# A 16-head attention block followed by a mixture of experts, float32 on one core: four heads per stack in row tiles of 32 rows, three score buffers, another order on VectorE and of the last up projections

## The chip, the cores and the metric

One core of a Trainium2 chip. The metric is the device time of one execution in microseconds. Three runs of the kernel before gave 1210.15, 1210.59 and 1213.12 us, median 1210.59.

## What is computed

The input x has 32 batches of 256 tokens with 128 features. Each batch passes a layer norm, attention with 16 heads of 8 features, a residual, a second layer norm, and four experts of 512 hidden features of which each token uses two, and a second residual. The attention weights are no softmax but `s(l - max l)` over its sum:

```python
pos = 1.0 + x * (1.0 + 0.5 * x * (1.0 + x / 3.0))
neg = 1.0 / (1.0 - x * (1.0 - 0.5 * x * (1.0 - x / 3.0)))   # x = logit - row maximum, so always this branch
h = silu(xf @ w1) * (xf @ w3)        # per expert
out = sum_e gates[:, e] * (h @ w2)   # gates: softmax, top 2, renormalized
```

## The kernel before, in words

The program is a software pipeline over batches. `over_batches` (L237) gives every engine, for each n from -2 to 33, a first half and a second half; all engines execute their instructions in the order written, and semaphores tie them together. B = 32 batches, U = 8 score tiles of a batch, G = 4 groups of four heads, UP = 8 units of the up projection (each 2 of the 16 blocks of 128 hidden features), C = 2 blocks of 128 tokens.

**First half of n.** TensorE computes the "distances" of batch n (logit minus row maximum, cubic argument), `distances` (L918), tile by tile, and between them the up projections of batch n-2, each unit u as an `a` part (w1, `up_a_unit`) and a `b` part (w3, `up_b_unit`), six matmuls each at L867. It also makes the values of batch n+1 (L959), the last weighted values of batch n-1 (L883), and turns and projects the attention output of batch n-1 (L979, L990, L998). ScalarE squares each distance tile (`square`, L498) and takes the silu of each `a` part (L506). VectorE forms the cubic `polynomial(u)` (L628) from the square and the distance and multiplies silu and `b` part (`hidden(u)`, L620). GpSimd splits queries and keys into a high and a low part (L393, L396), then waits for `gate_all`, the gates laid over all partitions by DMA, and multiplies the eight hidden units by them (`gate_hidden`, L384): seven in the first half, the eighth in the second half behind the wait for VectorE's layer norm statistics (`agg_ok`, L411). The `a` part has one PSUM bank (`up_a`), the `b` part is in `up_b`, for units 3, 5 and 7 in `pv`.

**Second half of n.** TensorE computes the raw scores of batch n+1 (`scores`, L1013) between the down projections of batch n-2 (`down(e, c)`, L1031, four blocks of an expert by w2, which as float32 are eight matmul records). VectorE takes the negated row minima of each score tile (`scores_max`, L718; the keys carry a minus sign, so these are the maxima), splits them (L769, L771), adds the expert result to the residual (`experts_added`, L744), and forms the router's logits, ranks and gates of batch n-1 (L751 to L805). The maxima are transposed on TensorE (`maxima_T`, L1078), copied out (`maxima_out`, L779), and written by a DMA of the SP queue (L347) into rows of the stacked queries, so that the distance matmul subtracts them. ScalarE does logarithm and exponential of the polynomials (L555, L560); TensorE multiplies the weights by the values (`weighted_values`, L870). At the end come the operand of the router (L1052), the operand and the projection of the queries and keys of batch n+2 (L1060, L1089), and the `a` and `b` part of unit 0.

Heads are stacked over partitions: a stack holds two heads in two halves of 64 rows, of which 60 (score) or all (distance, with the other head's rows of `k_pad` at zero) are used. A score tile has four matmuls, in two row tiles of 64 rows; a distance tile has four matmuls of all 128 rows. The stacks are filled from a scratch tensor in DRAM by the SP queue (12 DMAs a batch, L326 and L333). Scores and distances share two buffers of two PSUM banks each (`sc[:, u % 2, :]`), so a score tile u waits until tile u-2 has been reduced:

```python
pe.wait_ge(s_used, U * m + u - 1)      # scores(u), L1022
pe.wait_ge(hid_ok, UP * (m + 1) - 1)   # down(0, 0), L1037: units 0 to 6 are multiplied
pe.wait_ge(gated, UP * m + FB // 2 * (e + 1))   # down(e, c), L1040
```

VectorE's order in the first half is, for u = 0 to 7: `hidden(0)` ahead of `polynomial(0)`, the copy of the values ahead of `polynomial(1)`, the statistics of the next input ahead of `polynomial(3)`, `normalized` behind `hidden(3)`, `attention_added` ahead of `polynomial(7)`, and `hidden(u)` behind `polynomial(u)`. In the second half: statistics, the eight maxima with `router_T` and `queries_T` ahead of the seventh and `biased_logits` ahead of the eighth, `split_maxima`, `experts_added`, `shifted_logits`, `maxima_out`, `compare`, the copy of queries and keys, the gate steps.

## Time and profile before

| | us |
|---|---|
| median of three runs | 1210.59 |
| the profiled execution's own time | 1212.56 |
| its span, first to last instruction | 1210.8 |
| TensorE matmul busy | 1134.5 (94%) |
| ScalarE busy | 1001.7 (83%) |
| VectorE busy | 997.0 (82%) |
| GpSimd busy | 730.1 (60%) |

The profile is of one execution. Busy shares of TensorE are those of pipelined matmuls, whose records overlap: a group of matmuls is read from the start of one group to the start of the next. "Down pair" and the like below are names of stretches between two such starts. Times within the span count from its first instruction.

### The profile page before, as it was taken

To read this page: it belongs to the slowest core of one execution; us is meant where nothing else is said; L and a number is where in the kernel's file an instruction comes from. 1 tells how busy PE (TensorE), PEld (TensorE's weight loads), DVE (VectorE), ACT (ScalarE), POOL (GpSimd) and SP (SyncE) were. 2 spreads that over 40 slices of the span, in tenths; PEclk is the share of its full clock that TensorE was granted. 3 is DMA by queue.
4 is the path that set the end of the run, shared out by engine and by line. 5 is a ranking of instruction groups with operands and counts; after the bars stand their busy time and mean duration, and the time that the engine had idled before them with its cause. 6 is when DMAs were issued, how large, how long until landed. Compare 5 with 4: busy or idle time off the path is not lost.

```text
span 1210.8 us, 29497 instructions
## 1 busy us (share of the span) xinstructions
PE 1134.5 (94%) x10116; PEld 984.2 (81%) x10116; DVE 997.0 (82%) x1838; ACT 1001.7 (83%) x1001; POOL 730.1 (60%) x959
## 2 busy tenths in 40 slices
PE   2679999999999999999999999999999999999988
PEld 1447888888888888888888888888888888888877
DVE  5778888988888898888889888888988888898732
ACT  1378898888889888888988888998888889888862
POOL 6114666665656666565666656567666565766555
PEclk9988999999999999999999999999999999999999
DMA  5212212222221122222112222211222221122000
GB/s 177 64 62 79 63 51 65 79 84 84 84 63 48 61 78 84 84 83 65 49 59 78 84 84 84 67 55 50 78 84 84 84 68 54 50 78 81 28 23 27
DMA packets 92907, 84.89 MB, mean 70 GB/s; under 512 B 11784, under 2 KB 87240, under 8 KB 92872
## 3 DMA queue, kind: packets, MB, share of 16 engines
q1 hardware_dynamic: 92152, 83.79, 22.0%
q10 hardware_dynamic: 720, 0.66, 0.2%
q8 instruction: 20, 0.33, 0.1%
q14 instruction: 15, 0.12, 0.0%
HBM read 62.20 MB, written 21.10 MB: 69 GB/s over the span
## 4 chain that ended last, share of the span: by engine, by line
PE 62%; POOL 9%; issue 9%; DVE 8%; DMA 5%; ACT 3%; DVEq 2%; SPq 1%; ACTq 0%; POOLq 0%
PE up L867 18%; PE up L1042 10%; PE sc L933 9%; PE pv L883 9%; POOL hid L384 6%; DVE mx L718 4%; PE sc L1026 4%; DMA gate_all<-gate_scratch 3%; PE pv L867 3%; DVEq L709 2%; POOL xn L436 2%; PE misc L1094 1%; PE misc L1075 1%; DVE poly L628 1%; ACT silu_a L506 1%
## 5 line engine op out<-in xcount | busy, mean ns | idle before, releaser
L384 POOL TENSOR_TENSOR hid<-hid,gate_all 128x512 f32<-128x512 f32 x256 | 403.0, 1615 | 201.2 <-DMA gate_all<-gate_scratch 157.4
L498 ACT ACTIVATE w_sq<-sc 128x1024 f32<-128x1024 f32 x256 | 259.4, 1027 | 140.2 <-PE sc L933 138.6
L628 DVE SCALAR_TENSOR_TENSOR poly<-w_sq,sc 128x1024 f32<-128x1024 f32 x256 | 311.7, 1218 | 58.0 <-ACT w_sq L498 49.4
L718 DVE TENSOR_REDUCE mx<-sc 128x4 f32<-128x1024 f32 x256 | 299.7, 1214 | 32.2 <-PE sc L1026 30.7
L1042 PE MATMUL up<-w_sb,hid 128*128 128x128 f32 x2048 | 269.8, 281 | 0.6 <-POOL hid L384 0.6
L867 PE MATMUL up<-xn_hi,w_hi 128*128 128x256 f32 x832 | 253.8, 305 | 2.2 <-ACT silu_a L506 1.5
L555 ACT ACTIVATE poly<-poly,two 128x2048 f32<-128x2048 f32 x128 | 254.9, 1991 | 0.4
L1042 PEld LDWEIGHTS up<-w_sb,hid 128*128 128x128 f32 x2048 | 243.0, 192 | 12.5 <-POOL hid L384 0.8
L560 ACT ACTIVATE poly<-poly 128x2048 f32<-128x2048 f32 x128 | 242.6, 1896 | 0.0
L867 PE MATMUL up<-xn_hi,w_lo 128*128 128x256 f32 x832 | 234.2, 282 | 0.0
L867 PE MATMUL up<-xn_lo,w_hi 128*128 128x256 f32 x832 | 233.5, 281 | 0.0
L933 PE MATMUL sc<-q_stack,k_pad 128*128 128x256 f32 x1024 | 168.6, 293 | 9.4 <-DVE poly L628 6.4
L506 ACT ACTIVATE silu_a<-up 128x512 f32<-128x512 f32 x256 | 153.1, 598 | 26.3 <-PE up L867 19.6
L867 PEld LDWEIGHTS up<-xn_hi,w_hi 128*128 128x128 f32 x832 | 156.9, 189 | 19.0 <-issue 13.5
L933 PEld LDWEIGHTS sc<-q_stack,k_pad 128*128 128x128 f32 x1024 | 140.1, 194 | 27.7 <-issue 12.2
L867 PEld LDWEIGHTS up<-xn_lo,w_hi 128*128 128x128 f32 x832 | 157.4, 189 | 0.8
L867 PEld LDWEIGHTS up<-xn_hi,w_lo 128*128 128x128 f32 x832 | 156.0, 187 | 0.0
L1026 PE MATMUL sc<-k_pad,q_stack 60*128 60x256 f32 x1024 | 111.5, 326 | 40.7 <-DVE mx L718 23.8
L883 PE MATMUL pv<-poly,v_pad 128*32 128x256 f32 x2048 | 134.8, 393 | 2.3 <-ACT poly L560 2.3
L1026 PEld LDWEIGHTS sc<-k_pad,q_stack 60*128 60x128 f32 x1024 | 75.7, 196 | 67.5 <-DVE mx L718 34.9
L620 DVE TENSOR_TENSOR hid<-silu_a,up 128x512 f32<-128x512 f32 x160 | 109.1, 682 | 14.7 <-PE up L867 7.7
L883 PEld LDWEIGHTS pv<-poly,v_pad 128*32 128x32 f32 x2048 | 57.7, 111 | 45.2 <-ACT poly L560 4.2
(100 smaller groups left out, 1382.0 us busy)
## 6 DMA issues: line engine op xcount, KB each, us to landing
qk_scratch<-qk_split SPq DMA_DIRECT2D x32, 512.0 KB, 3.5
gate_all<-gate_scratch SPq DMA_DIRECT2D x32, 512.0 KB, 5.2
k_pad<-qk_scratch SPq DMA_DIRECT2D x254, 64.0 KB
q_stack<-qk_scratch SPq DMA_DIRECT2D x124, 128.0 KB
x_in<-in_L_attn_x_dram SPq DMA_DIRECT2D x32, 128.0 KB, 2.1
x_res<-in_L_attn_x_dram SPq DMA_DIRECT2D x32, 128.0 KB, 2.3
out_dram<-y_acc SPq DMA_DIRECT2D x32, 128.0 KB, 2.2
poly<-in_L_ffn_w_dram SPq DMA_DIRECT2D x2, 1024.0 KB, 6.9
```

The source lines that it names most:

```text
L384: nc.gpsimd.tensor_tensor(h, h, by_token.unsqueeze(1).to_broadcast([128, 2, C, 128]), ALU.mult).then_inc(gated, 1)
L498: nc.scalar.activation(w_sq[:, u % 2, :], sc[:, u % 2, :], ACT.Square).then_inc(sq_ok, 1)
L506: nc.scalar.activation(silu_a[:, u % 2, :], up_a[:], ACT.Silu).then_inc(silu_ok, 1)
L555: nc.scalar.activation(poly[:, C * g:C * (g + 1), :], poly[:, C * g:C * (g + 1), :], ACT.Ln, bias=two[:]).then_inc(ln_ok, 1)
L560: nc.scalar.activation(poly[:, C * g:C * (g + 1), :], poly[:, C * g:C * (g + 1), :], ACT.Exp, scale=-1.0).then_inc(p_ok, 1)
L628: nc.vector.scalar_tensor_tensor(poly[:, u, :], w_sq[:, u % 2, :], 3.0, sc[:, u % 2, :], ALU.add, ALU.mult).then_inc(poly_ok, 1)
L718: nc.vector.tensor_reduce(by_row[:, :, 2 * g:2 * g + 2], sc[:, u % 2, :].rearrange("p (j k t) -> p j k t", j=2, k=2), AX.X, ALU.min, negat ...
L867: last = nc.tensor.matmul(dst, lhs[a], rhs[b], start=(k == 0), stop=(k == len(terms) - 1))
L883: last = nc.tensor.matmul(pv[32 * j:32 * j + 32, g // 2, :], v_pad[par][:, c, 4 * g + j, first:first + 32], poly[:, C * g + c, at:at + S], ...
L933: last = nc.tensor.matmul(sc[:, u % 2, at:at + S], k_pad[par][:, 2 * g + k, j, c * 128:(c + 1) * 128], q_stack[par][:, 2 * g + k, :], star ...
L1026: last = nc.tensor.matmul(sc[:, u % 2, at:at + S], q_stack[par][rows, 2 * g + k, c * 128:(c + 1) * 128], k_pad[par][rows, 2 * g + k, j, :] ...
L1042: last = nc.tensor.matmul((up_b, up_a)[c][:, 0:D], hid[:, FB * e + f, c * 128:(c + 1) * 128], w2_sb[:, FB * e + f, :], start=(e == 0 and f ...
```

## The change

`TILE = 32`, `STEP = 4`: a stack now holds four heads in four row tiles of 32 rows (24 rows of queries or keys, and two rows for the maxima), `q_stack` and `k_stack` have G = 4 instead of 8 positions, and the zeros of `k_pad` are gone. Score and distance matmuls each use one row tile. `scores(g)` writes two tiles at once, eight matmuls in four row tiles, and rotates through three buffers, the third of which (`spare`) lies in the banks of `up_a` and `pv`. The order of the down projections is by token block first: (0,0), (0,1), score 0, (0,2), (0,3), score 1, (1,0) and so on, all in the bank `up_b`. On VectorE `hidden(6)` and `hidden(7)` come behind `polynomial(7)`; the copy of the values goes to ScalarE; the input's statistics go to the end of the second half, with a load of x three batches ahead; `queries_T` and `biased_logits` go behind the maxima; `experts_added` goes behind `shifted_logits`. On TensorE the last up projections run as a6, distance 7, a7, b6, b7; `maxima_T` comes behind the `a` part of unit 0. The expert weights are loaded later in the start, through `hid` instead of `poly`, and their low parts are formed on GpSimd. Seven DMAs a batch fill the stacks. The steady loop ends one pair of batches earlier.

```diff
-                    if u < 2:
-                        after(pe, poly_ok, U * m - 1 + u)
-                        if u == 0:
-                            pe.wait_ge(stacked[par], pair_count(i, off + 1, STACKED))
+                    if g == 0:
+                        after(pe, poly_ok, U * m)
+                        pe.wait_ge(stacked[par], pair_count(i, off + 1, STACKED))
                     else:
-                        pe.wait_ge(s_used, U * m + u - 1)
-                    for k in range(2):
-                        for j in range(2):
-                            at, rows = (2 * j + k) * S, slice(HALF * j, HALF * j + 60)
...
+                        if g == 1 and has(i, off - 2):
+                            pe.wait_ge(hid_ok, UP * (n - 1))
+                        if g == 1 and has(i, off - 1):
+                            pe.wait_ge(o_ok, n)
+                        pe.wait_ge(s_used, U * m + 2 * g - 1)
+                    for c in range(C):
+                        for h in range(4):
+                            rows, at = slice(TILE * h, TILE * (h + 1)), (C * (h % 2) + c) * S
+                            op = nc.tensor.matmul(score_buf[2 * g + h // 2][:, at:at + S],
+                                                  q_stack[par][rows, g, c * 128:(c + 1) * 128],
+                                                  k_stack[par][rows, g, :], start=True, stop=True)
+                            if c == C - 1 and h % 2:
+                                op.then_inc(s_full, 1)
...
+                for c in range(C):
+                    for h in (2 * (u % 2), 2 * (u % 2) + 1):
+                        last = distance_of(i, off, u // 2, h, c)
...
                 down(0, 0)
+                down(0, 1)
                 score(0)
+                down(0, 2)
+                down(0, 3)
                 score(1)
-                down(0, 1)
                 down(1, 0)
+                down(1, 1)
                 score(2)
+                down(1, 2)
+                down(1, 3)
                 score(3)
...
-                ups(6)
+                if has(i, off - 2):
+                    up_a_unit(i, off - 2, 6)
                 distance(7)
-                ups(7)
+                if has(i, off - 2):
+                    up_a_unit(i, off - 2, 7)
+                    up_b_unit(i, off - 2, 6)
+                    up_b_unit(i, off - 2, 7)
...
-                    if u > 0 and has(i, off - 2):
+                    if 0 < u < U - 2 and has(i, off - 2):
                         hidden(u)
...
+                if has(i, off - 2):
+                    hidden(U - 2)
+                    hidden(U - 1)
...
                 if has(i, off + 1):
                     split_maxima()
+                if has(i, off - 1):
+                    biased_logits()
+                    shifted_logits()
                 if has(i, off - 2):
                     experts_added()
-                if has(i, off - 1):
-                    shifted_logits()
                 if has(i, off + 1):
                     maxima_out()
+                if has(i, off + 2):
+                    queries_T()
```

In the new `down(c, e)` the wait for `hid_ok` stands ahead of (0,0) and the wait for `gated` ahead of all four (0,e). `up_a_unit` is unchanged and waits, for unit 0, for `acc_ok` of the same half, which `experts_added` gives.

## Rows read from the trace of the kernel before

**Rows 1.** The page's head: span, and busy time by engine

```profile
span 1210.8 us, 29497 instructions
...
PE 1134.5 (94%) x10116; PEld 984.2 (81%) x10116; DVE 997.0 (82%) x1838; ACT 1001.7 (83%) x1001; POOL 730.1 (60%) x959
```

**Rows 2.** Timeline of TensorE: first distances of batches 2, 16 and 30 (start us, us, what)

```profile
105.52 1.19 PE L933 MATMUL sc<-q_stack,k_pad 128*128 128x256 f32 x8
...
600.01 1.21 PE L933 MATMUL sc<-q_stack,k_pad 128*128 128x256 f32 x8
601.06 0.61 PE L959 MATMUL misc<-proj_T,xn_T 128*128 128x128 f32 x4
...
1093.49 0.71 PE L933 MATMUL sc<-q_stack,k_pad 128*128 128x256 f32 x4
```

**Rows 3.** Timeline of TensorE from 580 to 625 us

```profile
581.87 1.05 PE L1042 MATMUL up<-w_sb,hid 128*128 128x128 f32 x8
582.86 0.74 PE L1026 MATMUL sc<-k_pad,q_stack 60*128 60x256 f32 x8
583.52 2.05 PE L1042 MATMUL up<-w_sb,hid 128*128 128x128 f32 x16
586.67 0.51 PE L1026 MATMUL sc<-k_pad,q_stack 60*128 60x256 f32 x4 [0.63 <-DVE mx L718]
587.10 2.05 PE L1042 MATMUL up<-w_sb,hid 128*128 128x128 f32 x16
...
596.24 0.40 PE L1085 MATMUL misc<-ident,mx_split 128*32 128x128 f32 x2
...
616.93 1.06 PE L1042 MATMUL up<-w_sb,hid 128*128 128x128 f32 x8
```

**Rows 4.** Timeline of VectorE, same stretch

```profile
581.16 0.48 DVE L663 TENSOR_TENSOR y_acc<-misc,x_resb 128x128 f32<-128x128 f32 x2
...
584.29 4.59 DVE L718 TENSOR_REDUCE mx<-sc 128x4 f32<-128x1024 f32 x4
...
593.99 1.22 DVE L718 TENSOR_REDUCE mx<-sc 128x4 f32<-128x1024 f32 x1
...
595.57 0.42 DVE L744 TENSOR_TENSOR y_acc<-up,y_acc 128x256 f32<-128x256 f32 x1
...
596.67 0.41 DVE L779 COPY m_split<-misc 32x256 f32<-32x256 f32 x1 [0.41 <-PE misc L1085]
...
599.76 0.89 DVE L805 TENSOR_TENSOR gates<-chosen,chosen_r 128x8 f32<-128x8 f32 x1
...
610.82 1.21 DVE L628 SCALAR_TENSOR_TENSOR poly<-w_sq,sc 128x1024 f32<-128x1024 f32 x1
...
612.54 1.21 DVE L628 SCALAR_TENSOR_TENSOR poly<-w_sq,sc 128x1024 f32<-128x1024 f32 x1
```

**Rows 5.** Timeline of GpSimd, then of the SP queue, same stretch

```profile
599.59 1.04 POOL L393 TENSOR_TENSOR qk_split<-qk,zero 128x512 fp32r<-128x512 f32 x1
...
608.69 11.01 POOL L384 TENSOR_TENSOR hid<-hid,gate_all 128x512 f32<-128x512 f32 x7 [6.70 <-DMA gate_all<-gate_scratch]
...
620.10 1.54 POOL L384 TENSOR_TENSOR hid<-hid,gate_all 128x512 f32<-128x512 f32 x1
...
602.76 0.46 SPq L318 DMA_DIRECT2D gate_all<-gate_scratch  x1
```

**Rows 6.** One tile, gate_all: what its DMAs took from issue to landing

```profile
DMA to landing us min/median/max: 3.6/5.2/7.0
```

**Rows 7.** The start: TensorE, then VectorE

```profile
27.09 1.22 PE L1026 MATMUL sc<-k_pad,q_stack 60*128 60x256 f32 x8 [13.12 <-DMA k_pad<-qk_scratch]
...
69.90 0.41 DVE L779 COPY m_split<-misc 32x256 f32<-32x256 f32 x1 [1.96 <-PE misc L1085]
```

**Rows 8.** The chain that ended last, its last pieces

```profile
1203.02 2.96 POOL hid L384 x2
1206.03 2.07 PE up L1042 x16
```

More of the change, by code:

```diff
@@ L177, in attention_then_experts_kernel @@
         m_ok = sem("m_ok")
-        ones_in = [sem(f"ones_in{i}") for i in range(2)]
         m_stacked = [sem(f"m_stacked{i}") for i in range(2)]
@@ L243, in over_batches @@
                 half_b(n // 2, n % 2)
[L244 removed]
+            with eng.Fori(2, B // 2 - 2) as i:
                 for off in range(2):
@@ L247, in over_batches @@
                     half_b(i, off)
-            for n in range(B - 2, B + 2):
+            for n in range(B - 4, B + 2):
                 half_a(n // 2, n % 2)
@@ L397, in first_half @@
                                             ALU.subtract).then_inc(qk_ok, 1)
+                if isinstance(i, int) and no(i, off) == 0:
+                    low_weights(0, w1_lo, w1_hi)
+                    low_weights(1, w3_lo, w3_hi)
                 if has(i, off - 2):
@@ L673, in first_half @@
                         hidden(0)
-                    if u == 1 and has(i, off + 1):
-                        values_copied()
-                    if u == 3 and has(i, off + 2):
-                        input_statistics()
                     if u == U - 1 and has(i, off - 1):
@@ L827, in second_half @@
                         router_T()
-                    if u == 6 and has(i, off + 2):
-                        queries_T()
-                    if u == 7 and has(i, off - 1):
-                        biased_logits()
                     if has(i, off + 1):
@@ L848, in second_half @@
                         gate_step(k)
+                if has(i, off + 3):
+                    input_statistics(n + 3)
             dve.wait_ge(consts_ok, 4)
@@ L878, in weighted_values @@
                         pe.wait_ge(hid_ok, UP * (n - 1))
+                    if has(i, off + 1):
+                        pe.wait_ge(s_used, U * (n + 1) + 6)
                 first = 16 - 16 * (g % 2)
@@ L948, in distance @@
                         distances(i, off, u)
-                distance(0)
-                distance(1)
+                if has(i, off):
+                    first_distances(i, off)
                 if has(i, off + 1):
@@ L961, in first_half @@
                     last.then_inc(v_full, 1)
+                if isinstance(i, int) and n == 1:
+                    weighted_values(i, off - 1, 2)
                 if has(i, off - 1):
@@ L1113, in second_half @@
                     queries_operand()
[L1114 to L1116 removed]
+                if isinstance(i, int) and n == 0:
+                    maxima_T()
+                if has(i, off):
+                    weighted_values(i, off, 0)
                 if has(i, off - 1):
                     router_logits()
[L1119 removed]
                 if has(i, off):
[L1121 removed]
                     weighted_values(i, off, 1)
[L1123 removed]
+                if has(i, off - 1):
+                    up_a_unit(i, off - 1, 0)
+                if has(i, off + 1) and not (isinstance(i, int) and n == 0):
                     maxima_T()
                 if has(i, off - 1):
[L1126 removed]
+                    up_b_unit(i, off - 1, 0)
                 if has(i, off + 2):
                     queries_and_keys()
[L1129 to L1131 removed]
+                if has(i, off) and not (isinstance(i, int) and n == 0):
                     weighted_values(i, off, 2)
```

254 lines of the change are left out of this document (115 added, 139 removed).

## The prediction

> **What bounds the kernel now.** The page comes first [rows 1]: TensorE has matmuls in flight for 94% of the span, so one expects a kernel that gets faster by what TensorE is spared. ScalarE and VectorE at 82 to 83% warn that they have little room. The timeline of TensorE then gives the period: from the first distances of batch 2 at 105.52 to those of batch 30 at 1093.49 are 28 batches, 35.28 us each [rows 2]. I cut the period at two points, F, the first distances (600.01), and D, the first down projection (581.87 and 616.93) [rows 2, 3]: F to D is 16.92 us; D to F, 581.87 to 600.01, is 18.14.
>
> From D to F the chain is this. VectorE starts the maxima at 584.29, D + 2.42, and eight of them take 1.15 us each (four in 4.59); the eighth starts at 593.99 [rows 4]. TensorE waits 0.63 us for them once, at 586.67 [rows 3]. The maxima are transposed at 596.24, copied out by 597.08, D + 15.21, and F follows 2.93 us later [rows 2 to 4]: that is the DMA which lays them into the stack. In the other half TensorE runs nearly without a gap. So the second half is a chain VectorE, TensorE, DMA, and only the first is TensorE's.
>
> A third path has slack today: the gates are done at 600.65 [rows 4], `gate_all` is issued at 602.76, the seven gated units run from 608.69 to 619.70 and the eighth from 620.10 to 621.64 [rows 5], 21.0 us behind the gates. The down projections that need it are the last two, some 9 us behind D, so they are not late.
>
> **The change on TensorE.** A score group of eight matmuls in two row tiles takes 0.66 us (582.86 to 583.52), one of four 0.43 (586.67 to 587.10) [rows 3]. The difference, 0.23 for two beats of two matmuls, leaves 0.20 for entering and leaving the tiled mode. A new score group has eight matmuls in two beats of four row tiles: 0.43 if four tiles run side by side, 0.66 if only two do. The trace shows two, so these are the ends; I take 0.43, since the tiles have their own banks. Eight times 0.33 become four times 0.43: 0.9 us less a batch. The first distances fall from 1.05 (eight matmuls one after another, 600.01 to 601.06 [rows 2]) to 0.43; the other six tiles are two beats of two, 0.43 against four full matmuls of 0.12, 0.47. That is 0.6 and 0.2, together 1.7 us of 35.3. The Trainium skill (TensorEngine Tiling, Key Properties) says that a change of tiling mode drains the engine; the 0.20 us agrees. Its table of theoretical speedups gives up to 4x for a contraction of 32; by it the six later tiles would save 6 x 0.35 = 2.1 us, by the rows 0.2, and I go by the rows: two tiles side by side, and a switch each way.
>
> **F to D.** VectorE loses the copy of the values and moves two statistics (together some 0.9 us), but the statistics now stand ahead of `hidden(0)`, and the gates are later against F (below). I walked the half through: b2 must wait for `hidden(1)` at F + 4.5 to 5.0, and `polynomial(4)`, which begins at F + 10.81 before [rows 4], begins at F + 10.1 (ends 9.9 and 10.3). From there VectorE has no gap: three times `polynomial` and `hidden` together, 1.72 each (610.82 to 612.54), `polynomial(7)` alone, some 1.13, and `attention_added`, 0.48 [rows 4], 6.8 us in all. `hidden(6)` now comes behind `polynomial(7)`, and down(0,0) must wait for it. So D is F + 16.9. TensorE, by its own work, would be there at F + 16.2; b6 and b7 behind a7 are covered, and a7 has a gap of 0.4 us, since the silu that frees `up_a` is covered by a distance tile alone. The half gains nothing.
>
> **D to F.** Score 0 stands behind two down projections instead of one: 1.98 us, twice the 0.99 from 581.87 to 582.86 [rows 3]. Its first tile can be read some 0.55 us later (0.43 and the way to VectorE), so the maxima begin at D + 2.53; VectorE is ready at D + 1.4 and waits. Before it was D + 2.42. Down(0,3) needs all eight gated units: statistics at D + 1.4, two small operations, and one gated unit of 1.54 [rows 5] make D + 3.5 at the earliest, against TensorE's own D + 3.4. Then score 1 comes at D + 4.5, 0.2 us too late for VectorE; score 2 costs it 0.1; the two operands behind score 3 cost it 0.6 ahead of `router_T`. Taken out are `queries_T` and `biased_logits`, together about 0.5. The maxima end at D + 13.1, before at 595.14, D + 13.27. Behind them are now the split (0.33), bias, shift (0.7 with their waits), and only then `experts_added` (0.42): a0 on TensorE, which waits for it, starts at D + 14.5, after 1.6 us of idle TensorE, and `maxima_T` stands behind a0 (0.72). The transpose is at D + 15.2 against 596.24, D + 14.37 [rows 3]. Copy (0.84 from the transpose's start) and DMA (2.93) bring F to D + 19.0, 0.9 us later than now. What TensorE was spared is spent waiting.
>
> **The gates.** `queries_T` behind `maxima_out`, the projection (1.14 to its copy), the copy and the steps give gates at D + 19.2 to 20.0. The spread is the last step: it takes 0.89 us and ends as GpSimd's first pass over the queries does, 599.59 to 600.63 [rows 4, 5], as if VectorE were held off; whether it slips in ahead decides. Gates to the end of the eighth unit: 2.1 to the issue, a landing of 5.2 (3.6 to 7.0 [rows 6]), 11.0, 0.4 and 1.54, in all 20.2 [rows 5]. Down(0,3) is D + 3.5 of the next batch, so the loop by this path is 15.7 to 16.5 + 20.2 = 35.9 to 36.7; a landing of 7 costs 1.8 more that once. The x load no longer goes ahead of `gate_all`, which may take up to 0.5 off.
>
> **The sum of a period** is 16.9 + 19.0 = 35.9 by the maxima and about as much by the gates; where two such loops meet, the later decides each time, so I add 0.25 and take 36.15, 0.87 more than now: 28 x 0.87 = +24 us.
>
> **Start and end.** The first scores wait until 27.09 for stacks [rows 7], behind 3 MB of expert weights and 12 loads; now there are 7 and the weights come after. I estimate 5.5 us less (2 to 8). In the two batches without experts the matmuls take twice as long, and the tiles save there: some 1.6 us; the transpose of batch 1's maxima no longer waits 1.96 us [rows 7], and the third weighted values are moved: 1.9 more. Start: -9 us (-13 to -4). GpSimd's two passes for the low weights, some 9 us, stand in idle time. At the end 1203.02 + 2.96 gates the last units, and 16 matmuls follow, 2.07 us [rows 8]; now five units of 0.99 follow, +3, and one more for the batch before: +4.
>
> Sum: 1210.8 - 9 + 24 + 4 = 1230 for the span. The profiled execution had 1212.56 for 1210.8; the median of the runs is 2 us under that, so the median comes out at **1230**.
>
> **Rivals.** *TensorE is the bound* and gets 1.7 us a batch back, less half for waits: the 94% speak for it, the gap of 0.63 us as the only one in its chain against. 28 x 0.85 = 24 off and 5 by the ends: 1182. *Faster a little*: the last gate step slips in ahead of GpSimd, so that `hidden(0)` and all of VectorE's first half come 0.8 us sooner. The price is paid at D: from `polynomial(4)` at F + 9.4 on, TensorE's own work (F + 16.2) sets D, the period is 16.2 + 19.0 = 35.2, and start and end make 1210.8 - 28 x 0.08 - 5 = 1204; with a landing 0.5 shorter, or a0 less late than walked, 1195. Against it: the step sits behind GpSimd's pass in the row. *No change*: period 35.45, +5 and -5; 1211. *Slower by more*: four row tiles do not run side by side (+0.23 for each score group, on VectorE's chain) or late landings cost 1.7 us every third time: period 36.9, 1251. *The code does not do what it says*: the third buffer could be of no use, because score 1 stands behind down(0,3); that is in the main case already.
>
> **Chances.** Main case 0.5, slower by more 0.12, no change 0.08, a little faster 0.2, TensorE bound 0.1. The bound of 0.3% (3.6 us), about what a measurement of this kernel can tell from no change, splits them: faster 0.30, same 0.08, slower 0.62. The main case alone has 1218 to 1242. For 8 in 10 the range must reach into the faster cases: 1190 to 1250.
>
> **What the new profile would show.** Right: a period near 36.1; D at F + 16.9 with the first down projection waiting for `hidden(6)`; maxima from D + 2.5; a wait of about 1.6 us of TensorE for `experts_added` ahead of a0; F at copy-out + 2.95; down(0,3) released by GpSimd in part of the batches; first scores near 21.5. Wrong: TensorE without gaps behind D, maxima that begin by D + 2.0, or score groups longer than 0.5 us.

## The result: 1271.58 us, 5.0% slower, and the profile after

Four runs of the changed kernel gave 1270.59 to 1272.57 us, median 1271.58; the kernel before, run beside it, has 1210.78. The ratio is 1.0498 (95% interval 1.048 to 1.0517). The prediction was 1230 with a range up to 1250: slower, as forecast, but 61 us slower instead of 19.

The head of the page after, then the first scores from the timeline of TensorE:

```profile
span 1269.5 us, 29119 instructions
...
PE 1135.1 (89%) x10116; PEld 911.3 (72%) x10116; DVE 985.9 (78%) x1804; ACT 1006.8 (79%) x1033; POOL 724.0 (57%) x961
```

```profile
19.97 0.80 PE L1049 MATMUL sc<-k_stack,q_stack 32*128 32x256 f32 x8 [7.04 <-DMA q_stack<-no_maxima]
```

Against [rows 1] no engine is busier than before by more than 5.1 us (ScalarE), and all shares fell: the engines wait more. Cut at the down projections (D) as in the prediction, the spans differ like this:

| stretch | before | after | difference | predicted |
|---|---|---|---|---|
| to the first D | 122.3 | 114.4 | -7.9 | -9 |
| 28 periods | 988.0 | 1049.4 | +61.4 | +24 |
| the rest | 100.5 | 105.7 | +5.2 | +4 |
| span | 1210.8 | 1269.5 | +58.7 | +19 |

So start and end went as worked out (the first scores start at 19.97 where the prediction has 21.5), and the loss is in the period. It has two sizes: 37.2 us in most batches and some 38.1 in 8 of 29. First a batch with 37.2, TensorE's timeline from D (638.37) over F (657.25) to the next D (675.63), a period of 37.26:

```profile
638.37 2.05 PE L1064 MATMUL banks<-w_sb,hid 128*128 128x128 f32 x16 [0.35 <-DVE hid L643]
640.35 0.51 PE L1049 MATMUL sc<-k_stack,q_stack 32*128 32x256 f32 x8
640.79 2.29 PE L1064 MATMUL banks<-w_sb,hid 128*128 128x128 f32 x16
...
653.09 0.36 PE L874 MATMUL banks<-xn_hi,w_hi 128*128 128x256 f32 x1 [1.60 <-DVE y_acc L753]
...
653.88 0.38 PE L1103 MATMUL misc<-ident,mx_split 128*32 128x128 f32 x2
...
657.25 0.51 PE L931 MATMUL sc<-q_stack,k_stack 32*128 32x256 f32 x8
...
675.63 2.05 PE L1064 MATMUL banks<-w_sb,hid 128*128 128x128 f32 x16 [0.36 <-DVE hid L643]
```

The idle 1.60 us ahead of the `a` part of unit 0 and the wait for `hidden(6)` at D are the two that were forecast. D to F is 18.88 here. F to D is 18.38, where [rows 2, 3] have 16.92. VectorE and GpSimd show what fills it:

```profile
657.82 0.90 DVE L813 TENSOR_TENSOR gates<-chosen,chosen_r 128x8 f32<-128x8 f32 x1
658.63 0.48 DVE L633 BATCH_NORM_STATS2 stats<-x_in 128x6 f32<-128x128 f32 x2
659.03 0.67 DVE L643 TENSOR_TENSOR hid<-silu_a,banks 128x512 f32<-128x512 f32 x1
...
668.09 1.21 DVE L651 SCALAR_TENSOR_TENSOR poly<-w_sq,sc 128x1024 f32<-128x1024 f32 x1
...
672.00 1.22 DVE L651 SCALAR_TENSOR_TENSOR poly<-w_sq,sc 128x1024 f32<-128x1024 f32 x1 [0.37 <-ACT w_sq L515]
673.14 0.48 DVE L679 TENSOR_TENSOR y_acc<-misc,x_resb 128x128 f32<-128x128 f32 x2
673.76 1.22 DVE L651 SCALAR_TENSOR_TENSOR poly<-w_sq,sc 128x1024 f32<-128x1024 f32 x1
674.90 1.28 DVE L643 TENSOR_TENSOR hid<-silu_a,banks 128x512 f32<-128x512 f32 x2
...
678.16 1.23 DVE L727 TENSOR_REDUCE mx<-sc 128x4 f32<-128x1024 f32 x1 [1.13 <-PE sc L1049]
```

```profile
657.64 1.04 POOL L407 TENSOR_TENSOR qk_split<-qk,zero 128x512 fp32r<-128x512 f32 x1
...
665.23 9.46 POOL L391 TENSOR_TENSOR hid<-hid,gate_all 128x512 f32<-128x512 f32 x6 [5.17 <-DMA gate_all<-gate_scratch]
675.66 1.53 POOL L391 TENSOR_TENSOR hid<-hid,gate_all 128x512 f32<-128x512 f32 x1 [0.97 <-DVE hid L643]
...
677.58 1.54 POOL L391 TENSOR_TENSOR hid<-hid,gate_all 128x512 f32<-128x512 f32 x1
```

The gates end at 658.72, D + 20.35 and F + 1.47, where [rows 2, 4] have F + 0.64. Only then come the statistics and `hidden(0)`, and with them all of VectorE's first half: the next D is 16.91 behind the gates. The eighth unit is multiplied at 679.12, 20.40 behind the gates, and the fourth down projection follows at 679.19, D + 3.56, with score 1 behind it (by TensorE's own work it would be D + 3.4). What makes the eighth unit late is VectorE: GpSimd has done six units at 674.69, stands 0.97 us for `hidden(6)` and does the seventh to 677.19, and the statistics, which stand behind `hidden(7)` and without which it may not take the eighth, end at 677.03, 18.31 behind the gates. So in the changed kernel one loop runs from batch to batch: **gates, statistics of the input and `hidden(0)`, VectorE's first half up to `hidden(6)`, `hidden(7)` and the next statistics, the eighth gated unit, down(0,3), score 1, maxima, `experts_added`, the `a` part, transpose, the copies and comparisons behind it, GpSimd's ranks and its pass over the queries, gates**. Cut at D it is 16.9 + 20.3 = 37.2. F is not a link of it. The DMA of the maxima lands 0.45 us ahead of F in a regular batch, and TensorE comes to F from its own matmuls without a gap.

A batch with 38.1 has D at 600.26. TensorE's timeline, then the windows (length in us, PE, PEld, DVE, ACT and POOL busy with instructions, granted TensorE clock, DMA share, GB/s):

```profile
615.03 0.55 PE L874 MATMUL banks<-xn_hi,w_hi 128*128 128x256 f32 x1 [1.66 <-issue]
...
616.46 0.63 PE L1103 MATMUL misc<-ident,mx_split 128*32 128x128 f32 x2
620.25 0.51 PE L931 MATMUL sc<-q_stack,k_stack 32*128 32x256 f32 x8
```

```profile
612.00:615.00 3.00, 1.38 (x20) 0.71 (x19) 2.80 (x9) 2.21 (x4) 0.87 (x2) 1.00 0.00 0
615.00:618.20 3.20, 3.17 (x15) 3.08 (x16) 1.08 (x6) 3.17 (x3) 0.00 (x0) 0.50 0.00 0
618.20:621.00 2.80, 2.80 (x31) 1.70 (x31) 1.46 (x5) 0.56 (x2) 2.48 (x8) 0.96 0.19 59
```

Behind the idle 1.66 us the granted clock is 0.50 (1.2 of 2.4 GHz) for at least the 3.2 us from 615.0 to 618.2, a matmul of the `a` part takes 0.24 instead of 0.133 us, the transpose is at D + 16.2 instead of 15.5, and F at D + 20.0 instead of 18.85. Seven of the eight long periods are of this kind. The eighth, from D at 226.05 on, has the full clock and a late landing, which is the only time in these batches that F waits long for its DMA:

```profile
246.43 0.51 PE L931 MATMUL sc<-q_stack,k_stack 32*128 32x256 f32 x8 [1.46 <-DMA q_stack<-m_split]
```

### The profile page after: what moved, and what is told of

Its sections match the earlier page's. It is cut to its first block, busy times and chain, and to the rows that moved or that the text cites. A ratio compares the mean times of both kernels' runs of the same rounds, so it can differ in the third digit from the quotient of the medians.

```text
span 1269.5 us, 29119 instructions
## 1 busy us (share of the span) xinstructions
PE 1135.1 (89%) x10116; PEld 911.3 (72%) x10116; DVE 985.9 (78%) x1804; ACT 1006.8 (79%) x1033; POOL 724.0 (57%) x961
## 4 chain that ended last, share of the span: by engine, by line
PE 64%; DVE 15%; issue 12%; ACT 4%; DMA 2%; POOL 1%; DVEq 1%; SPq 0%; POOLq 0%; ACTq 0%
PE banks L874 21%; PE banks L1064 20%; PE sc L931 5%; PE banks L892 5%; DVE mx L727 4%; DVE hid L643 4%; PE sc L1049 3%; ACT w_sq L515 3%; DVE poly L651 2%; PE misc L1112 2%; PE misc L1015 2%; PE misc L1113 1%; PE misc L996 1%; POOL hid L391 1%; PE banks L1049 1%
## 5 line engine op out<-in xcount | busy, mean ns | idle before, releaser
L874 PE MATMUL banks<-xn_hi,w_hi 128*128 128x256 f32 x1024 | 324.4, 317 | 64.0 <-issue 28.5
L874 PE MATMUL banks<-xn_lo,w_hi 128*128 128x256 f32 x1024 | 293.4, 287 | 0.0
L874 PE MATMUL banks<-xn_hi,w_lo 128*128 128x256 f32 x1024 | 292.9, 286 | 0.0
L874 PEld LDWEIGHTS banks<-xn_hi,w_hi 128*128 128x128 f32 x1024 | 197.6, 193 | 117.9 <-issue 75.9
L1064 PE MATMUL banks<-w_sb,hid 128*128 128x128 f32 x2048 | 268.0, 283 | 13.6 <-DVE hid L643 10.7
L1064 PEld LDWEIGHTS banks<-w_sb,hid 128*128 128x128 f32 x2048 | 240.0, 191 | 37.4 <-DVE hid L643 17.4
L874 PEld LDWEIGHTS banks<-xn_lo,w_hi 128*128 128x128 f32 x1024 | 198.8, 194 | 0.0
L874 PEld LDWEIGHTS banks<-xn_hi,w_lo 128*128 128x128 f32 x1024 | 198.0, 193 | 0.0
L643 DVE TENSOR_TENSOR hid<-silu_a,banks 128x512 f32<-128x512 f32 x256 | 171.3, 679 | 18.2 <-PE banks L874 15.2
L523 ACT ACTIVATE silu_a<-banks 128x512 f32<-128x512 f32 x256 | 154.3, 603 | 30.1 <-PE banks L874 24.9
```

Of the source, the lines that this page charges most:

```text
L523: nc.scalar.activation(silu_a[:, u % 2, :], up_a[:], ACT.Silu).then_inc(silu_ok, 1)
L643: nc.vector.tensor_tensor(hid[:, 2 * u:2 * u + 2, :].rearrange("p a t -> p (a t)"), silu_a[:, u % 2, :], b_bank[u], ALU.mult).then_inc(hid ...
L874: last = nc.tensor.matmul(dst, lhs[a], rhs[b], start=(k == 0), stop=(k == len(terms) - 1))
L1064: last = nc.tensor.matmul(up_b[:, c * D:(c + 1) * D], hid[:, FB * e + f, c * 128:(c + 1) * 128], w2_sb[:, FB * e + f, :], start=(e == 0 an ...
```

## The experiments

Twelve kernels. E2, e3, e4, e6 and e7 undo one or two moves of the change, e8 all that are orders; e5 and e12 also move one operation on GpSimd, e9 adds matmuls, e10 and e11 start from e8, and e1 changes the kernel before. Each is compared with the kernel before, whose median was 1209.43 (e1 to e4), 1209.39 (e5 to e8) and 1210.61 us (e9 to e12) beside them.

### e1: the narrower distance tiles alone, in the kernel before

```diff
-                        at = (2 * j + k) * S
+                        at, rows = (2 * j + k) * S, slice(HALF * j, HALF * (j + 1))
...
-                                                k_pad[par][:, 2 * g + k, j, c * 128:(c + 1) * 128],
-                                                q_stack[par][:, 2 * g + k, :], start=True, stop=True)
+                                                k_pad[par][rows, 2 * g + k, j, c * 128:(c + 1) * 128],
+                                                q_stack[par][rows, 2 * g + k, :], start=True, stop=True)
```

The last operation of the cubic is a maximum in place of a product here; it takes 1.22 us a tile, as before.

> The kernel before, with only the distance matmuls put into two row tiles of 64 rows (two beats of two, as the changed kernel has them from tile 2 on). This leaves the maxima of every second head out of the distances, and the cubic takes a maximum in place of its last product so that its logarithm stays defined. Theory A (each tile pays for the mode on both sides: in the changed kernel a distance and two up units come every 2.06 us, before every 1.91): six tiles cost 0.15 us each, the first two together save 0.2, F to D grows by 0.7 us, 28 batches: about 1230 us. Theory B (the terms of the prediction, 0.43 for a tile against 0.47): F to D shrinks by 0.4 to 0.6 and the time goes to about 1195 us, or stays where VectorE takes over.

Measured: 1213.22 us, ratio 1.0037 (1.0022 to 1.0052). F to D is 17.25 instead of 16.90. Two neighbouring tiles on TensorE:

```profile
606.80 0.28 PE L867 MATMUL pv<-xn_hi,w_lo 128*128 128x256 f32 x1
607.01 0.50 PE L933 MATMUL sc<-q_stack,k_pad 64*128 64x256 f32 x4
607.45 0.39 PE L867 MATMUL up<-xn_hi,w_hi 128*128 128x256 f32 x1
607.67 0.28 PE L867 MATMUL up<-xn_lo,w_hi 128*128 128x256 f32 x1
...
609.07 0.50 PE L933 MATMUL sc<-q_stack,k_pad 64*128 64x256 f32 x4
```

The group itself takes 0.44 start to start, as the prediction read it. But the matmul ahead of it takes 0.21 and the first behind it 0.22, where one takes 0.12 between its like. A tile and its two up parts so come every 2.06 us instead of 1.91. Between up projections, narrower tiles for a group of four so cost 0.15 us instead of saving 0.04; only the first group of eight gains (1.31 instead of 1.59 us from F to the weighted values). The sign is the first theory's, the size, 0.35 us in the half, is half of its 0.7. The traces show where the rest is. From tile 3 to 4 the kernel before needs 2.00 us and not 1.91, and from tile 5 to 6, beside the transposes, 2.29 where e1 needs 2.23; from tile 2 to tile 7 e1 is 0.47 us slower and not 0.75. And D to F became 0.2 us shorter (18.13 instead of 18.32 in the median batch), so that the period grew by 0.11 us only, from 35.28 to 35.39. In the kernel before, narrower tiles are nearly free: the 4 us are a fifth of what the first theory expected.

### e2: `hidden(6)`, `hidden(7)` and the last up projections in their old order

```diff
-                    if 0 < u < U - 2 and has(i, off - 2):
+                    if u > 0 and has(i, off - 2):
...
-                if has(i, off - 2):
-                    hidden(U - 2)
-                    hidden(U - 1)
...
-                if has(i, off - 2):
-                    up_a_unit(i, off - 2, 6)
+                ups(6)
                 distance(7)
-                if has(i, off - 2):
-                    up_a_unit(i, off - 2, 7)
-                    up_b_unit(i, off - 2, 6)
-                    up_b_unit(i, off - 2, 7)
+                ups(7)
```

> The changed kernel, with the last up projections back to a6, b6, distance 7, a7, b7 and hidden(6), hidden(7) back to their places behind polynomial(6) and polynomial(7). Theory A (the first down projection waits for hidden(6) behind polynomial(7), and the maxima begin 2.53 us behind it): D comes 1 us sooner against F, until the loop over the gates (36.2 us) binds: about 1245 us. Theory B (the slower distance tiles set F to D by the squares, and the place of hidden(6) is not what D waits for): at most 0.3 us a batch, 1263 us or more.

Measured: 1270.15 us, ratio 1.0509 (1.0485 to 1.0534), no change against the changed kernel. Yet both halves moved: F to D 17.52 instead of 18.37, D to F 19.71 instead of 18.85. TensorE's timeline, then its chief wait (us, times, longest):

```profile
637.07 1.95 PE L1057 MATMUL banks<-w_sb,hid 128*128 128x128 f32 x16
...
641.46 1.16 PE L1057 MATMUL banks<-w_sb,hid 128*128 128x128 f32 x8 [0.92 <-POOL hid L391]
```

```profile
PE banks L1057 <- POOL hid L391: 32.0, 33, 1.8
```

D came 0.85 us sooner and down(0,3) waited 0.92 for its gated unit: it starts at D + 4.39, which is 20.47 behind the gates, exactly as in the changed kernel. Which wait ends last had changed, the loop had not: VectorE's statistics end 18.38 behind the gates, where the changed kernel has 18.31, since the order of `hidden(6)`, `hidden(7)` and `polynomial(7)` among themselves does not change when the last of them is done.

### e5: e2, and the eighth gated unit ahead of the wait for the statistics

```diff
+                if has(i, off - 2):
+                    gate_hidden(no(i, off) - 2, UP - 1)
                 lo, hi = (0 if has(i, off - 1) else C), (2 * C if has(i, off + 2) else C)
...
-                if has(i, off - 2):
-                    gate_hidden(no(i, off) - 2, UP - 1)
```

> The changed kernel with the last up projections and hidden(6), hidden(7) as before, which alone brought D 0.85 us sooner and the time not at all, and now also GpSimd's eighth gated unit ahead of its wait for the statistics. Theory A (one loop holds the kernel: gates, VectorE's first half, eighth gated unit, down(0,3), score 1, maxima, gates; what came sooner at D was waited off at down(0,3)): down(0,3) starts by gates + 19.5 instead of 20.5, the period falls from 37.3 to about 36.3 and the time to about 1243 us. Theory B (the gain at D is lost on VectorE or in the operands behind the maxima, not at down(0,3)): less than 0.3 us a batch, 1262 us or more.

Measured: 1234.51 us, ratio 1.02 (1.0163 to 1.0237). Down(0,3) is 19.38 behind the gates instead of 20.47, the period 36.04, and the wait of e2 has shrunk:

```profile
PE banks L1057 <- POOL hid L391: 3.3, 4, 1.8
```

1.1 us taken from that one link came out of each period. This is the run that shows the loop: what e2 took from D and what this takes from GpSimd are worth nothing and 36 us, in that order. It was 8 us better than expected (1243), nearly all by the regular period, 36.04 where 36.3 was expected (28 x 0.26 = 7). Six half-clock batches are left, with 36.8, where e2 has nine.

### e3: the transpose of the maxima ahead of the `a` part

```diff
-                if has(i, off - 1):
-                    up_a_unit(i, off - 1, 0)
                 if has(i, off + 1) and not (isinstance(i, int) and n == 0):
...
+                if has(i, off - 1):
+                    up_a_unit(i, off - 1, 0)
```

> The changed kernel, with the transpose of the maxima back ahead of the a part of up unit 0 on TensorE. Theory A (the transpose waits for experts_added through a0, and TensorE's idle 1.66 us there lets the clock fall in 7 of 28 batches): F comes 0.7 us sooner, and no batch runs a0 at half the clock any more, 28 x 0.7 + 6 = 26 us: about 1246 us. Theory B (D to F is held by the way of the queries and keys or the weighted values behind it): no more than the 6 us of the clock, 1265 us.

Measured: 1240.16 us, ratio 1.0243 (1.0222 to 1.0264). In a regular batch the transpose is at D + 13.8, F at D + 18.2, F to D 17.94 and the period 36.15, 1.07 less. That half-clock batches would vanish was a miss: the clock still falls in 8, which now take 37.7. The idle time is only cut in two by the transpose, while the `a` part waits for `experts_added` as before:

```profile
601.81 0.40 PE L1103 MATMUL misc<-ident,mx_split 128*32 128x128 f32 x2 [0.74 <-DVE mx_split L779]
602.72 0.36 PE L874 MATMUL banks<-xn_hi,w_hi 128*128 128x256 f32 x1 [0.52 <-issue]
```

### e4: each score group one down projection sooner

```diff
                 down(0, 0)
-                down(0, 1)
                 score(0)
+                down(0, 1)
                 down(0, 2)
-                down(0, 3)
                 score(1)
+                down(0, 3)
                 down(1, 0)
-                down(1, 1)
                 score(2)
+                down(1, 1)
                 down(1, 2)
-                down(1, 3)
                 score(3)
...
+                down(1, 3)
```

> The changed kernel, with each score group one down projection sooner (score 0 behind down(0,0), score 1 behind down(0,2) and ahead of down(0,3), which waits for the gates, and so on), and the two operands ahead of the last down projection. Theory A (the maxima begin at D + 2.53 because score 0 stands behind two down projections, and VectorE's chain behind them sets F): maxima from D + 1.55, F 1.2 us sooner, about 1237 us. Theory B (F is held by TensorE's own work or by the loop over the gates): less than 0.4 us a batch, 1260 us or more.

Measured: 1229.59 us, ratio 1.0161 (1.0144 to 1.0178), 42 us under the changed kernel and 7 under what was expected. Maxima from D + 1.63 instead of 2.53 (down projection at 584.61), F at D + 17.7, gates at D + 19.2, period 36.1, no half-clock batch:

```profile
586.25 2.35 DVE L727 TENSOR_REDUCE mx<-sc 128x4 f32<-128x1024 f32 x2 [0.24 <-PE sc L1049]
```

The wait of VectorE for the first scores was 1.13 and is 0.24. Down(0,3) with its late gated unit now stands behind score 1 and no longer holds it.

### e6: `shifted_logits` behind `experts_added` again

```diff
                     biased_logits()
-                    shifted_logits()
                 if has(i, off - 2):
                     experts_added()
+                if has(i, off - 1):
+                    shifted_logits()
```

`biased_logits` stays ahead: the router's logits lie in the bank of the down projections' output, which the next `b` part overwrites.

> The changed kernel with experts_added between biased_logits and shifted_logits, so that a0 can start 0.37 us sooner. Theory A (a0 waits for experts_added and the transpose of the maxima stands behind a0, all on the one loop): period less by 0.35 to 0.4, 10 us, and fewer falls of the clock: 1256 to 1261 us. Theory B (the way holds elsewhere): 1268 us or more.

Measured: 1252.82 us, ratio 1.0347 (1.031 to 1.0384). The `a` part starts at D + 14.37 instead of 14.77, the period is 36.83 instead of 37.2, and the clock falls in two batches instead of eight. Two small operations of 0.16 and 0.17 us on VectorE (L767 and L770) were worth 19 us, since they stood ahead of the one that TensorE waited for, in every batch: 11 by the regular period, the rest by the clock and the late landing, which this run does not have.

### e7: e3 and e4 together

```diff
+                down(1, 3)
...
+                if has(i, off - 1):
+                    up_a_unit(i, off - 1, 0)
```

These are the last lines of the two diffs above; the rest of both stands as shown there.

> The changed kernel with the scores one down projection sooner and the transpose of the maxima ahead of a0, which alone gave 42 and 31 us. Theory A (both lie one after the other on the same loop, gates to D 16.9 us, D to gates 20.3): D to gates falls to 18.1, period 35.0, about 1198 us. Theory B (the two cover each other, or TensorE's own work takes over): 1220 us or more.

Measured: 1199.49 us, ratio 0.9906 (0.9874 to 0.9938), expected 1198. The period is 35.0: from 37.2, e3 takes 1.07 and e4 1.14, and both together 2.2. They are links of one chain, which add up. Had they been two ways side by side, of which the later decides, the savings would not have added up.

### e8: all orders undone

The diffs of e2, e3, e4 and e6 together, of which this is the shortest:

```diff
-                    shifted_logits()
                 if has(i, off - 2):
                     experts_added()
+                if has(i, off - 1):
+                    shifted_logits()
```

The four-head stacks, the third buffer, the copy of the values on ScalarE, the moved statistics and the new start stay.

> The changed kernel with row tiles, three score buffers and the moves of the values, the statistics and the start kept, and all orders put back: last up projections, hidden(6) and (7), the scores one down projection sooner, the transpose of the maxima ahead of a0, shifted_logits behind experts_added. Theory A: gates to D 16.1, maxima from D + 2.4 because VectorE then is the late one, D to gates 18.5, period 34.6, about 1188 us, under both kernels. Theory B (the row tiles and the third buffer cost as much as they bring, so that only the orders count): 1205 to 1212 us.

Measured: 1193.90 us, ratio 0.9858 (0.983 to 0.9885): faster than both kernels, though 1188 with a period of 34.6 was expected. The head of its page, then TensorE's timeline of one batch (D at 602.78):

```profile
span 1193.7 us, 29119 instructions
...
PE 1109.4 (93%) x10116; PEld 894.2 (75%) x10116; DVE 968.5 (81%) x1804; ACT 1000.8 (84%) x1033; POOL 727.6 (61%) x961
```

```profile
602.78 1.05 PE L1058 MATMUL banks<-w_sb,hid 128*128 128x128 f32 x8
...
607.19 2.05 PE L1058 MATMUL banks<-w_sb,hid 128*128 128x128 f32 x16 [0.44 <-POOL hid L391]
...
616.43 0.36 PE L872 MATMUL banks<-xn_hi,w_hi 128*128 128x256 f32 x1
...
619.90 0.51 PE L929 MATMUL sc<-q_stack,k_stack 32*128 32x256 f32 x8
```

The `a` part starts with no idle time ahead of it, F is D + 17.1, F to D 17.73, the period 34.85. The gates are at D + 18.15 where 18.5 was expected, but from there to D it is 16.7 and not 16.1; e12 shows what holds it.

### e9: the idle time filled

Twelve matmuls that nobody reads, into the free bank, ahead of the `a` part:

```diff
+                    for _ in range(12):
+                        nc.tensor.matmul(up_a[:, 0:S], w1_hi[:, 0, 0:128], w3_hi[:, 0, 0:S], start=True, stop=True)
                     up_a_unit(i, off - 1, 0)
```

> The changed kernel with twelve more matmuls of 256 columns on TensorE, between weighted_values(1) and a0, into the bank that a0 then overwrites: work of 1.4 us in an idle stretch of 1.66. Theory A (the batches of 38.1 us differ from those of 37.2 by the clock alone, which falls behind the idle stretch): no a0 at half rate, all periods 37.2 to 37.3, 8 x 0.85 = 7 us less: about 1264 us. Theory B (those batches are slow for another reason): 1271 us, or more if the twelve delay a0.

Measured: 1264.04 us, ratio 1.0438 (1.0419 to 1.0458), expected 1264. The `a` part still starts at D + 14.77 and all periods are 37.2 to 37.3. Timeline and windows of one batch:

```profile
615.38 1.68 PE L1142 MATMUL banks<-w_hi 128*128 128x256 f32 x12
617.11 0.36 PE L874 MATMUL banks<-xn_hi,w_hi 128*128 128x256 f32 x1
```

```profile
614.50:617.00 2.50, 2.50 (x28) 1.78 (x25) 2.36 (x9) 1.71 (x3) 0.53 (x1) 1.00 0.00 0
617.00:619.50 2.50, 2.33 (x17) 2.04 (x17) 1.09 (x7) 2.48 (x2) 0.02 (x1) 1.00 0.00 0
```

The granted clock stays at 1.00 in every batch where 8 had fallen to 0.50. So the idle time ahead, and not the position in the program, made the clock fall. The run is 7.5 us faster by the medians, 28 x 0.25 = 7 by the periods; 1 of the 7 is the late landing, which this run does not have, and 6 are the clock (7 x 0.9).

### e10: e8 with two score buffers

```diff
-        score_buf = [(sc[:, 0, :], sc[:, 1, :], spare)[u % 3] for u in range(U)]
+        score_buf = [sc[:, u % 2, :] for u in range(U)]
...
-                        pe.wait_ge(s_used, U * m + 2 * g - 1)
+                        pe.wait_ge(s_used, U * m + 2 * g)
```

> The kernel with all orders undone, with two score buffers instead of three, each score group waiting for both tiles before it. Theory A (the third buffer is what lets a group of eight matmuls in four row tiles run beside VectorE): score 1, 2 and 3 wait for the second tile before, VectorE stands 0.55 us three times, period 34.9 + 1.7, about 1240 us. Theory B (the buffer is of no use here, since VectorE waits for other things): within 5 us of 1194.

Measured: 1235.40 us, ratio 1.0209 (1.019 to 1.0228), period 35.95. VectorE waits 0.60 us for every new pair:

```profile
559.84 2.36 DVE L724 TENSOR_REDUCE mx<-sc 128x4 f32<-128x1024 f32 x2 [0.60 <-PE sc L1043]
```

The third buffer is worth 41 us here: 28 periods of 1.1 are 31, and the first D is 8.6 us later. The period was expected at 36.6: D to F grew by the expected 1.7 us, from 17.16 to 18.86, but F to D fell by 0.6. The prediction called the buffer of no use as long as score 1 stands behind down(0,3). For e8's order that is refuted; in the order of the changed kernel it was not tried. There score 1 starts at 643.01 and the second maximum, for which two buffers would make it wait, ends at 643.25. The Trainium skill (TensorEngine Tiling, PSUM Bottleneck) warns that tiling speeds up TensorE but not the emptying of PSUM. The trace agrees: a pair is written in 0.44 us and read in 2.3, so what counts is how early the next pair can be written.

### e11: e8 with the other distance tiles in pairs too

Tiles 2 and 3, 4 and 5, 6 and 7 as eight matmuls in four row tiles each, so that fewer groups enter and leave the tiled mode:

```diff
+                if u % 2:
+                    return
...
-                pe.wait_ge(poly_ok, U * m + u - 1)
+                pe.wait_ge(poly_ok, U * m + u)
                 for c in range(C):
-                    for h in (2 * (u % 2), 2 * (u % 2) + 1):
-                        last = distance_of(i, off, u // 2, h, c)
-                last.then_inc(w_full, 1)
+                    for h in range(4):
+                        op = distance_of(i, off, u // 2, h, c)
+                        if c == C - 1 and h % 2:
+                            op.then_inc(w_full, 1)
```

> The kernel with all orders undone, with distance tiles 2 and 3, 4 and 5, 6 and 7 written together in four row tiles, as 0 and 1 are, so that TensorE changes its mode 3 times less in the first half. Theory A (a change of mode costs TensorE some 0.2 us on either side and F to D is TensorE's and VectorE's together): TensorE is spared 1.9 us, VectorE waits at the third pair, F to D 0.5 us shorter, 1180 us. Theory B (the ping-pong of tiles between TensorE, ScalarE and VectorE is worth more than the mode changes): F to D longer by 0.5 us or more, 1205 us or above.

Measured: 1220.19 us, ratio 1.0076 (1.006 to 1.0093), period 35.5, in the second theory's range. F to D grew from 17.73 to 18.3. VectorE's timeline and its wait for the squares in the whole run, here and in e8:

```profile
569.88 1.22 DVE L651 SCALAR_TENSOR_TENSOR poly<-w_sq,sc 128x1024 f32<-128x1024 f32 x1 [1.15 <-ACT w_sq L515]
```

```profile
DVE poly L651 <- ACT w_sq L515: 96.8, 126, 1.9
```

```profile
DVE poly L651 <- ACT w_sq L515: 63.0, 129, 1.4
```

Three groups fewer a batch (0.44 us and 0.19 for the edges each) are dearly bought: with both buffers filled at once TensorE can't write while they are read, and square and cubic stand idle after each pair.

### e12: e8 with the eighth gated unit ahead

The edit of e5, on e8:

```diff
+                if has(i, off - 2):
+                    gate_hidden(no(i, off) - 2, UP - 1)
                 lo, hi = (0 if has(i, off - 1) else C), (2 * C if has(i, off + 2) else C)
...
-                if has(i, off - 2):
-                    gate_hidden(no(i, off) - 2, UP - 1)
```

> The kernel with all orders undone and GpSimd's eighth gated unit ahead of its wait for the statistics. Theory A (down(0,3) waits 0.44 us in this kernel, and VectorE 0.2 us for score 2 behind it): period 34.7 instead of 34.9, 1188 to 1191 us. Theory B (the wait is covered): 1193 to 1195.

Measured: 1193.09 us, ratio 0.9854 (0.9836 to 0.9872), the same as e8 within both intervals and in the second theory's range, with the same period of 34.85. The gates come at D + 17.65 instead of 18.15, but F to D takes 18.23 instead of 17.73. TensorE's wait for the cubic in the distances, here and in e8:

```profile
PE sc L929 <- DVE poly L651: 20.7, 37, 1.2
```

```profile
PE sc L929 <- DVE poly L651: 7.1, 10, 1.2
```

So the gated unit is no longer in the loop, and another one holds 34.85. The traces point to ScalarE. In e12 its two loads of function tables (ACT_TABLE_LOAD), the logarithms and exponentials and the silu of unit 0 follow each other without a gap from 563.69 to 582.22, and VectorE has the gates at 581.26 and stands for that silu:

```profile
581.62 0.60 ACT L523 ACTIVATE silu_a<-banks 128x512 f32<-128x512 f32 x1
...
582.30 0.69 DVE L643 TENSOR_TENSOR hid<-silu_a,banks 128x512 f32<-128x512 f32 x1 [0.64 <-ACT silu_a L523]
```

In e8 `hidden(0)` follows the same silu, 0.14 us after VectorE was ready, and stands at D + 18.72 as in e12. What sooner gates give is waited off there. No run shortened ScalarE's stretch, so this is read and not tested.

## Why the prediction was wrong

**Right.** Slower, and why: the maxima from D + 2.53, the idle 1.6 us ahead of the `a` part (1.60 to 1.66), `experts_added` as its releaser, and D waiting for `hidden(6)`. D to F is 18.85 against 19.0, but in its last piece that is luck: the copy of the maxima ends at D + 16.44 instead of 16.0, and F follows 2.44 us behind it and not 2.93, for in the changed kernel it does not wait for the DMA. Eight matmuls in four row tiles take 0.44 us (640.35 to 640.79), as the lower bound said. Start -7.9 against -9, end +5.2 against +4.

**The step that failed is F to D, 18.37 against 16.9.** It has two parts of about equal size in the batch shown. `polynomial(4)` starts at F + 10.84 instead of 10.1, and from there D takes 7.54 instead of 6.8.

The first 0.74 is the gates. The prediction put them at D + 19.2 to 20.0, which is F + 0.2 to 1.0; they end at D + 20.3, F + 1.5. From the gates to `polynomial(4)` it is 9.37 us, and the prediction's own numbers give 9.1 to 9.9. So VectorE's walk was right and started too early. The last gate step takes 0.90 us and again ends as GpSimd's pass over the queries does (658.72 and 658.68). That the eighth unit ends 20.4 behind the gates, where 20.2 was predicted, is luck too: the prediction's 20.2 ran over the landing of `gate_all` and GpSimd's eight units, and the trace has GpSimd waiting for VectorE. But the worse fault was one of method: the gates were carried forward only to the eighth unit, and F to D was held at its own value. The loop by the maxima and the loop by the gates were two candidates, with 0.25 us added "where two such loops meet". They were one loop. Whatever is late in D to gates moves the statistics, `hidden(0)`, D, the eighth unit and score 1 with it. E7 shows it by adding up, e2 and e5 by where a saved microsecond vanishes and where it doesn't.

The other 0.74 is TensorE's tile, a mis-sized term: 0.46 us more ahead of `polynomial(6)` for a square that waits for its tile (the row shows 0.37 of it as idle), 0.14 more around `attention_added`, and 0.14 in small pieces, chiefly from the end of `hidden(6)` to D. The reading of 0.43 us for a tile was right and its price wrong: the neighbours pay 0.09 and 0.10 more, as e1 shows, 2.06 instead of 1.91 from tile to tile, and the changed kernel has the same 2.06. In the changed kernel TensorE needs 7.70 us from the `b` part of unit 2, which waits for `hidden(1)`, to the tile of `polynomial(6)` (662.61 to 670.31), where the kernel before needs 7.34 (605.33 to 612.67) and the prediction's tiles would have needed 0.1 less than that. No run took the edges out of the changed kernel alone. The prediction cut a group out from start to start and so left its edges in the neighbours' account. By e1 the later tiles cost TensorE some 0.5 us a batch where they were to save 0.2, so 0.7 of the 1.7 us that it was to be spared was not there; in the changed kernel that is hidden in its waits.

**Not foreseen: the clock.** 7 of 28 periods are 0.9 us longer, since TensorE's clock is at half behind the idle time. The prediction forecast the idle time and priced it at its length only. E9 measures it, some 6 of its 7.5 us. Late landings, which the prediction named in a rival at 1.7 us every third time, came once, at 1 us.

The sum: from 35.28 to 37.22 in regular batches is 28 x 1.94 = 54 us, and the clock with the late landing is 7, together the 61.4 of the table. Of the 39.5 us between +19.2 and +58.7, F to D has 28 x 1.47 = 41, less 28 x 0.15 for D to F and 28 x 0.25 for the allowance that is now in it, plus 7 for the clock and the landing and 2 for start and end.

**The rivals.** "Slower by more", 1251 at a period of 36.9, was nearest, by other causes than its own: the four row tiles do run side by side. "TensorE is the bound" is refuted: orders alone (e8) take 78 us off with the same matmuls. That the third buffer was of no use is wrong for e8 (41 us, e10) and untested for the order as changed.

**What the change is made of.** Taken from the changed kernel one at a time: score groups sooner -42 us, transpose first -31, shifted logits -19, the order of `hidden` and up projections -1 (-37 with the gated unit ahead), all together -78. The single ones add up to 93, more than all together, since at 34.85 us another loop takes over (e12). What then remains of the change is 1.4% faster than before, and 2.1% slower if it has two score buffers (e10). How much of that belongs to the start, to the copy on ScalarE or to the moved statistics wasn't separated.

## What to carry to other kernels

Find the loop before adding up halves: follow one late result from its engine through every other until it reaches itself in the next batch, and carry each delay all the way round. An instruction that another engine waits for goes ahead of whatever nobody waits for; a few moves of order, each of some tenths of a microsecond to one, turned a gain of 1.4% into a loss of 5%. And price a mode switch by the whole cycle from group to group, not by the group.

## What the runs showed of the hardware

**Row tiles.** Eight matmuls with 32 rows in four row tiles take 0.44 us, with 60 rows in two 0.66 [rows 3]. Between up projections a group costs the matmul ahead of it 0.09 and the one behind it 0.10 us more (e1). A group of four in two beats (2.06 from tile to tile) therefore loses against four full matmuls (1.91), and a group of eight gains: from F to the weighted values 1.31 us in two row tiles and 1.09 in four (657.25 to 658.34) against 1.59.

**The clock behind short idle times.** With 1.6 us of idle ahead of the `a` part the granted clock fell from 1.00 to 0.50 in 8 of 29 batches (the seven above and the last one); with 0.74 and 0.52 us around a transpose (e3) in 8; with the same 1.6 us in e2 and e5 in 9 and 6; with some 1.2 us (e6) in 2; with 0.7 us in one piece (e4), with 0.4 (e7), with no idle time there (e8) and with the idle time filled (e9), in none. The Trainium skill (TensorE: Matmul & The Clock Gate, Part 1) says that a gate passes only a share of the clock's pulses, by how busy TensorE has been of late. The runs agree that idleness is the cause: 615.0 to 618.2 is at 0.50, and e9, with the idle time filled, has 1.00. Why only some batches fall, with the same idle time in all, no run here shows.

**VectorE's last gate step** takes 0.90 us and ends with GpSimd's pass over the queries, before and after, where another operation of the same size (L770) takes 0.17. The orders moved the two against each other. The step takes 0.89 us where it starts 0.17 behind the start of the 1.04 us pass (the kernel after, e4), 0.63 where it starts 0.43 behind (e3, e7) and 0.53 where it starts 0.53 behind (e8, e12), and in every trace it ends 0.02 to 0.03 us behind the end of the pass. So the end of GpSimd's pass, and not the step's own length, says when the gates are done. A step that met no pass at all is in no run.
